# Re-ordering the work ahead of the first head step in an AdaLN, attention and routed-FFN kernel

## The reference

```python
# block 1 (the part that the change touches)
scale, shift = split(emb @ W_emb + b_emb)
xn  = rms_norm(x, g_norm) * (1 + scale) + shift
q, k, v = heads(xn @ W_qkv)                 # 16 heads of 32
q, k = rms_norm(q, g_q), rms_norm(k, g_k)   # per head
o   = softmax(q k^T * 32**-0.5) v           # 512 x 512 per head, no mask
y   = o + o @ W_out
# block 2: latent attention with rotary parts and a causal mask
h   = y + attention(rmsnorm(y))
# block 3: one shared expert, and 2 of 7 routed experts per token
out = x + h + moe(rmsnorm(h))
```

## Time and profile before

| | |
|---|---|
| median of 3 runs | 1350.78 us (1350.34 to 1356.07) |
| the profiled execution | 1353.06 us |
| its span, first to last instruction | 1351.3 us |
| TensorE busy in the span | 1200.8 us (89%) |
| VectorE, ScalarE, GpSimd busy | 738.7, 576.2, 296.2 us |
| mean granted TensorE clock | 0.959 of full |

### The profile page before, as it was taken

The page is one execution under the profiler, slowest core; times in us unless marked ns, Lnnn a source line. Parts: engine busy times, 40 slices in busy tenths (PEclk is TensorE's granted clock), DMA queues, the critical chain, the costliest instruction groups (busy, mean ns, idle before and its releaser), DMA issues.

```text
span 1351.3 us, 18930 instructions
## 1 busy us (share of the span) xinstructions
PE 1200.8 (89%) x6315; PEld 860.4 (64%) x6315; DVE 738.7 (55%) x1548; ACT 576.2 (43%) x1248; POOL 296.2 (22%) x244
## 2 busy tenths in 40 slices
PE   4857989999999889999999989989988898999970
PEld 4734655665566456558668767766656687888860
DVE  4346386467545765655465375465354675444432
ACT  3215365435433554554454454454364653222210
POOL 2312222100210021001011100200124344555530
PEclk9968999999999999999999899998999998999995
DMA  6062243224311731442365263354448623655669
GB/s 244 1 187 91 74 133 109 79 76 161 110 45 63 229 95 48 145 157 76 109 204 165 67 206 122 83 192 139 123 161 298 212 86 94 110 110 110 111 125 332
DMA packets 88030, 178.43 MB, mean 132 GB/s; under 512 B 12512, under 2 KB 23168, under 8 KB 86400
## 3 DMA queue, kind: packets, MB, share of 16 engines
q1 hardware_dynamic: 79424, 157.29, 36.1%
q0 software_dynamic: 8512, 19.93, 7.9%
HBM read 111.64 MB, written 65.27 MB: 131 GB/s over the span
## 4 chain that ended last, share of the span: by engine, by line
PE 75%; DVE 10%; DMA 5%; ACT 4%; issue 4%; SPq 1%; POOL 1%; ACTq 0%; DVEq 0%; POOLq 0%
PE psum L841 13%; PE psum L658 9%; PE psum L660 7%; PE psum L659 7%; PE psum L825 6%; PE psum L801 6%; PE psum L667 3%; PE psum L918 3%; PE psum L920 3%; PE psum L919 3%; DVE nmax L1547 2%; PE psum L945 2%; PE psum L887 2%; PE psum L947 2%; PE psum L946 2%
## 5 line engine op out<-in xcount | busy, mean ns | idle before, releaser
L1137 ACT ACTIVATE probs<-psum 128x512 f32<-128x512 f32 (+3 forms) x512 | 256.3, 516 | 241.9 <-PE psum L828 128.3
L1547 DVE TENSOR_REDUCE nmax<-psum 128x1 f32<-128x512 f32 (+3 forms) x512 | 290.5, 585 | 120.9 <-PE psum L801 86.4
L825 PE MATMUL psum<-stack 97*128 97x512 f32 (+3 forms) x512 | 204.2, 400 | 27.5 <-ACT probs L1137 18.8
L801 PE MATMUL psum<-stack 96*128 96x512 f32 (+3 forms) x512 | 211.5, 418 | 6.4 <-DMA stack<-split_s 6.4
L841 PE MATMUL psum<-probs,vals 128*33 128x512 f32 (+3 forms) x1024 | 210.5, 533 | 0.0
L825 PEld LDWEIGHTS psum<-stack 97*128 97x128 f32 x512 | 99.6, 195 | 49.0 <-ACT probs L1137 27.2
L801 PEld LDWEIGHTS psum<-stack 96*128 96x128 f32 x512 | 101.2, 198 | 39.8 <-issue 28.4
L841 PEld LDWEIGHTS psum<-probs,vals 128*33 128x33 f32 x1024 | 49.6, 112 | 99.7 <-issue 69.3
L658 PE MATMUL psum<-w_hi,xh 128*128 128x512 f32 (+1 forms) x256 | 95.2, 372 | 7.3 <-POOL xl L1239 5.6
L659 PE MATMUL psum<-w_hi,xl 128*128 128x512 f32 (+1 forms) x256 | 93.6, 366 | 0.0
L660 PE MATMUL psum<-w_lo,xh 128*128 128x512 f32 (+1 forms) x256 | 93.6, 366 | 0.0
(11 more groups left out here) (236 smaller groups left out, 2372.5 us busy)
## 6 DMA issues: line engine op xcount, KB each, us to landing
stack<-split_s SPq DMA_DIRECT2D x384, 128.0 KB, 3.0
split_s<-split SPq DMA_DIRECT2D x64, 512.0 KB, 2.8
xt<-in_x_dram SPq DMA_DIRECT2D x4, 1024.0 KB, 5.8
x_s<-yt SPq DMA_DIRECT2D x4, 1024.0 KB, 5.0
xt<-x_s SPq DMA_DIRECT2D x4, 1024.0 KB, 4.8
yt<-in_x_dram SPq DMA_DIRECT2D x4, 1024.0 KB, 5.5
res<-x_s SPq DMA_DIRECT2D x4, 1024.0 KB, 9.6
acc_s<-yt SPq DMA_DIRECT2D x4, 1024.0 KB, 5.9
```

The lines of the kernel that those rows point to most:

```text
L801: last = nc.tensor.matmul(psum[:, bank, 0:n], st[:, 0, t * P:(t + 1) * P], st[:, 1, 0:n], start=True, stop=not causal)
L825: last = nc.tensor.matmul(psum[:, bank, lo:S], st[:, 1, t * P:(t + 1) * P], st[:, 0, lo:S], start=True, stop=not causal)
L1137: sk.cleared(nc.scalar.activation(probs[:, M % NX, lo:S], psum[:, sk.bank(M), lo:S], ACT.Exp, scale=SCALE), M)
L1547: sq.cleared(V.tensor_reduce(nmax[:, M // STEPS_P % 2, c:c + 1], psum[:, sq.bank(M), 0:n], AX.X, ALU.max, negate=True), M)
```

## The change

Six things change, all ahead of the first head step or in the first round.

1. All four low parts of Wqkv are made by VectorE, ahead of its wait for the modulation product. GpSimd makes none.
2. The first `qk` product no longer waits for all of x and Wqkv: before each of its four chunks TensorE waits for the chunk's x and low part alone.
3. Values later: after the `qk` products come `hnorm` and `hscale` of group 0, then `v` 0 to 2, `turn` q and `turn` k of group 0, `v` 3, then `hscale` and `turn` of group 1.
4. The RMS norm of sequence 1 moves from the head steps 4 to 11 of round 0 in among the `qk` products (after `qk` 2, 5 and 6); SP loads that x ahead of its stores.
5. Pair 0 is not read back from DRAM. SP and ScalarE copy it from `split` straight into `stack`, with 12 DMAs of 64 KB (SP head 0, ScalarE head 1; each 3 for k, 3 for q). The stores of group 0 still run, for pair 1. ScalarE waits for these 12 copies before it overwrites `split` with group 1.
6. `turn_max(0)` comes after `scores` 9 in place of after `scores` 13, and ScalarE issues the DMA of its row in place of SP.

Small things: the router weights' split moves to later points of `FIRST`.

```diff
@@ before_heads(j)
+    square, norm, scale = normalize(j + 1)
     for n in range(2 * NT):
         keys += [("qk", j, n)] + ([("hsum", j, n - 1)] if n else [])
-    keys += [("hsum", j, 2 * NT - 1)] + [("v", j, t) for t in range(NT)] + [("hnorm", j, n) for n in range(4)]
-    for g in range(2):
-        keys += [("hscale", j, g, c) for c in "kq"] + [("turn", j, g, c) for c in "kq"]
-    return keys
+        keys += {2: square, 5: norm, 6: scale}.get(n, [])
+    keys += [("hsum", j, 2 * NT - 1)] + [("hnorm", j, n) for n in range(4)] + [("hscale", j, 0, c) for c in "kq"]
+    keys += [("v", j, t) for t in range(NT - 1)] + [("turn", j, 0, c) for c in "qk"] + [("v", j, NT - 1)]
+    return keys + [("hscale", j, 1, c) for c in "kq"] + [("turn", j, 1, c) for c in "qk"]
@@ beside_heads(k)
     if k == 0:
-        square, norm, scale = normalize(j)
-        put((4, 5, 6, 7), square)
-        put((8, 8, 9, 9), norm)
-        put((10, 10, 11, 11), scale)
@@ waits on the stack
-            eng.wait_ge(stack_ld[p % 4], 96 * (p // 4 + 1))
+            eng.wait_ge(stack_ld[p % 4], 96 * (p // 4 + (1 if p % 4 else 2)))
+        FIRST_PARTS, FIRST_SIDE = {"k": {0: 2, 1: 2, 2: 3}, "q": {0: 0, 1: 1, 2: 0}}, {"k": 1, "q": 0}
@@ SP
+            def place_first(c):
+                for role in FIRST_PARTS[c]:
+                    sp.dma_start(stack[DH * role:DH * role + DH, FIRST_SIDE[c], 0, :].bitcast(F32),
+                                 split[0:DH, FIRST_PARTS[c][role], :].bitcast(F32)).then_inc(stack_ld[0], 16)
...
-            for g in range(2):
-                store_k(0, g)
-                store_q(0, g)
-                for a in range(2):
-                    load_pair(0, 2 * g + a)
             load_x(1)
-            place_rows(0)
+            store_k(0, 0)
+            place_first("k")
+            store_q(0, 0)
+            place_first("q")
+            load_pair(0, 1)
+            store_k(0, 1)
+            store_q(0, 1)
+            for q in (2, 3):
+                load_pair(0, q)
@@ TensorE
+            def first_chunk_ready(c):
+                pe.wait_ge(v_lo, VALUE_NO["x", 0, c] + 1)
+                pe.wait_ge(w1_lo, c + 1)
...
-                        product(key, tokens(t), w1(c * D, D))
+                        product(key, tokens(t), w1(c * D, D), None if at_[0] or j else first_chunk_ready)
...
             for M in range(LEAD):
                 scores(M)
-            turn_max(0)
+                if M == STEPS_P + 1:
+                    turn_max(0)
@@ ScalarE
                     g, c = at_
+                    if NG * j + g == 1:
+                        wait_stack(act, 0)
...
+            def place_first(c):
+                for role in FIRST_PARTS[c]:
+                    act.dma_start(stack[DH * role:DH * role + DH, FIRST_SIDE[c], 1, :].bitcast(F32),
+                                  split[DH:2 * DH, FIRST_PARTS[c][role], :].bitcast(F32)).then_inc(stack_ld[0], 16)
...
             for key in FIRST[NT:]:
                 beside(key)
-                if key == ("x", 0, NC - 1):
+                if key == ("turn", 0, 0, "k"):
+                    ring.wait_read(act, key)
+                    place_first("k")
+                    act.wait_ge(v_lo, VALUE_NO["turn", 0, 0, "q"] + 1)
+                    place_first("q")
+                if key == ("v", 0, 0):
                     act.wait_ge(rw_ok, 1)
                     copy(rwh[:, :, :], rwt[:, :, :]).then_inc(rw_hi, 1)
             max_rows(0)
+            ring.wait_read(act, ("max", 0))
+            act.dma_start(stack[XSTACK:XSTACK + 1, 0, 0:2, :].bitcast(F32).rearrange("a h (t c) -> a (h t) c", c=P),
+                          mrow[0:2 * NT, :].bitcast(F32)).then_inc(rows_ld[0], 16)
@@ GpSimd
-            for c in (1, 3):
-                pool.wait_ge(w1_hi, c + 1)
-                nc.gpsimd.tensor_tensor(w1l[:, c, :], w1_raw[:, c, :], w1h[:, c, :].bitcast(F32),
-                                        ALU.subtract).then_inc(w1_lo, 1)
@@ VectorE
             for key in FIRST[NT:3 * NT]:
                 beside(key)
+            for c in range(NC):
+                dve.wait_ge(w1_hi, c + 1)
+                V.tensor_tensor(w1l[:, c, :], w1_raw[:, c, :], w1h[:, c, :].bitcast(F32), ALU.subtract).then_inc(w1_lo, 1)
             dve.wait_ge(mod_mm, 1)
...
-            for c in (0, 2):
-                dve.wait_ge(w1_hi, c + 1)
-                V.tensor_tensor(w1l[:, c, :], w1_raw[:, c, :], w1h[:, c, :].bitcast(F32), ALU.subtract).then_inc(w1_lo, 1)
```

More of the change, by code:

```diff
@@ L653, in _, with three @@
         def _(pe):
-            def three(out, lhs, rhs):
+            def three(out, lhs, rhs, ready=None):
                 n = len(lhs)
                 for i, ((ah, al), (bh, bl)) in enumerate(zip(lhs, rhs)):
+                    if ready:
+                        ready(i)
                     nc.tensor.matmul(out, ah, bh, start=(i == 0), stop=False)
@@ L668, in turn, with product @@
                 ring.filled(last, key)
-            def product(key, lhs, rhs):
+            def product(key, lhs, rhs, ready=None):
                 ring.wait_free(pe, key)
                 n = rhs[0][0].shape[-1]
-                ring.filled(three(psum[:, ring.bank(key), 0:n], lhs, rhs), key)
+                ring.filled(three(psum[:, ring.bank(key), 0:n], lhs, rhs, ready), key)
+            def first_chunk_ready(c):
+                pe.wait_ge(v_lo, VALUE_NO["x", 0, c] + 1)
+                pe.wait_ge(w1_lo, c + 1)
             def chans():
@@ L713, in beside @@
                     if j < B:
-                        if at_[0] == 0:
+                        if at_[0] == 0 and j:
                             pe.wait_ge(v_lo, VALUE_NO["x", j, NC - 1] + 1)
-                            if j == 0:
-                                pe.wait_ge(w1_lo, NC)
-                        product(key, tokens(t), w1(c * D, D))
+                        product(key, tokens(t), w1(c * D, D), None if at_[0] or j else first_chunk_ready)
                     elif c == 0:
@@ L1572, in _ @@
                 beside(key)
-                if key == ("x", 0, NC - 1):
+                if key == ("hnorm", 0, 3):
                     dve.wait_ge(v2_ld, 64)
                     dve.sem_inc(rw_ok, 1)
+                if key == ("turn", 0, 0, "k"):
                     dve.wait_ge(rw_hi, 1)
```

## The result

The changed kernel takes 1329.23 us (median of 4 runs, 1327.75 to 1332.91) against 1350.71 for the kernel before: ratio 0.9836, interval 0.9804 to 0.9868. Timed again in five rounds it gave 0.9840 (0.9809 to 0.9872). The forecast was 1327, with 1322 to 1336 as its range. The profiled execution has a span of 1328.2 us; before it was 1351.3.

The account below looks back on a forecast made before the run. TensorE was taken to bound the whole run (89% busy), with holes at the front. Gains of 17.4 us up to scores_t(0) and 6.3 in round 0 sum to 23.7; from the median, 1350.78 - 23.7 = 1327, range 1322 to 1336.

Parts of the forecast that it names:

- Low parts: Wqkv low parts made before VectorE's wait for the modulation product: x starts at 29.3 in place of 32.28, 3.0 us gained.
- Chunks: First qk product by chunks: last chunk starts at 36.2, product ends at 37.3 in place of 43.7; 6.4 us gained so far.
- Values later: Before the head steps: turn q at 64.5, its low part ending at 68.2; the fourth v costs nothing.
- Direct copies: Pair 0 straight into the stack, 0.43 us per issue, landing 2.85: first scores at 74.1 in place of 85.5, 11.4 gained.
- Row of maxima: Row issued at 81.8, landing in 2.6 us: scores_t(0) at 84.4 in place of 101.8, 17.4 gained.
- rival B: Before scores_t(0), the row of maxima waits for the loads around it, landing in 5.67: 3.1 us less gain, 1330; chance 0.12.
- Round 0: Steps 0 to 17: shorter step 12 wait (3.8), less time at the lower clock (1.8), shorter VectorE queue (0.7): 6.3 us.
- A: Rival, pair 0's copies: ScalarE issues as slowly as GpSimd, 1.59 us each; scores 4.9 late, 1332; chance 0.10.
- C: Rival, steps 0 to 17 of round 0: nothing gained there, another wait fills step 12; 1333 us; chance 0.10.
- D: Rival: no change, the front's gain is taken back by a later wait that doesn't move; 1350 us; chance 0.03.
- E: Rival: slower, pair 0's direct copies are the bottleneck at 6.78 us per issue; scores 36 later, 1363; chance 0.03.
- the signs of being wrong: First scores after 79, over 4 us from the row's issue to scores_t(0), or over 2 us waiting on stack at step 2.

Follow-up runs that it names:

- The undoing run: Changed kernel with the RMS norm of sequence 1 again beside head steps 4 to 11 of round 0; scores_t(0) to first qk of sequence 1: 33.61 against 28.04 us.

## Why the prediction was right

The chain that it named was the right one. The gain, 21.5 us, lies 2.2 under its 23.7, but that closeness is in part luck. Up to Q, where the chain ends, the changed kernel gained 18.3 (18.9 in its repeat), 5 under the forecast. The rest came behind Q, where nothing was changed, and did not come again: from Q to the end it is 1217.1 before, 1212.3 in the changed kernel's first profile and 1218.0 in its repeat. Timed again, the medians differ by 19.6. By the prediction's own steps:

*Low parts (3.0 forecast).* x's first value at 29.58, 2.7 gained; undoing it cost 2.6.

*Chunks (3.4 more).* Undoing them cost 3.1 at C. What I had missed is in the row at 33.52: the first matmul waited 0.94 for VectorE, not for GpSimd. The product's bank is that of x's third transpose, and is free only when the third value has been read. I had the start at 32.1. From 33.52 on TensorE never waited for a chunk: seven steps of 0.43 kept it busy until each was there, so the last low part, which I had as the limit, was not one here. It was in the three profiles in which all of the product's matmuls took 0.23. There TensorE waited between the chunks, as in the run with pair 0 through DRAM:

```profile
36.70 0.50 PE L666 MATMUL psum<-w_hi,xh 128*128 128x512 f32 x1 [0.28 <-POOL xl L1258]
```

This is the last chunk (36.2 forecast), and C was 37.7, only 0.4 earlier. The gain at C was 5.8, not 6.4.

*Values later.* `turn` q came 27.0 after C; 27.2 had been worked out from the end of the first product. The fourth `v` lay in idle time; worth 2.4.

*Direct copies: the step that failed.* I took 0.43 for an issue on both queues and let 1.7 us come from skipping DRAM (5.0 forecast between C and the first scores, less 2.7 for the fourth `v` and 0.6 for GpSimd's quicker low part). The issues took 0.51 to 1.88, 0.88 on average on ScalarE. The 512 KB stores between the copies are a part of it, as the run with the copies first shows: ScalarE's six took 5.26 with them and 4.12 without, where I had 2.6. The first scores came 8.8 earlier, not 11.4, and the new wait behind them put the first maximum 1.64 behind the scores in place of 0.80 (I had allowed 2.1). Together the part cost 1.1 to 1.8 where I had counted on a small gain. The range for the price of ScalarE's issue, 0.43 to 1.59, held it (0.88).

*Row of maxima.* `turn_max` and the changed queue are worth 3.9, the x load's new place 1.9. The landing took 3.7 where I took 2.6, inside the bounds 2.4 to 5.67. The prediction's "six more" maxima was wrong, though its sum, which goes by the 93.65 of the row, does not use it. Here rival B had the mechanism, and with it the rule quoted from the Trainium skill ("DMA: Bandwidth & Descriptors", "Issuing engines are not separate DMA queues"). With the loads of pairs 2 and 3 kept away the row landed 1.8 sooner; so they held it up, though it was issued from another queue, and issued by SyncE it landed no later (3.65). The trace agrees with the rule. The same rule says that issuing from two engines saves only issue time; 12 copies issued in 4.1 us, against 12 loads in 5.5 on one queue, do not speak against it.

*Round 0.* 6.3 forecast. The undoing run gives 5.6 to 7, with the 3.60 wait to the hundredth. In the changed kernel's own profile only 4.4 showed; its repeat had a stretch of 26.8, which makes it 5.6. The term was some 0.7 too large, or more.

The terms at T, from the runs: low parts 2.6, chunks 2.7, values 2.4, row of maxima 3.9, x load 1.9, direct copies -1.8: together 11.7 of the 13.9 that T moved. Some 0.5 of the rest is GpSimd's low part of q, 1.29 where it was 1.83; the other 1.7 was not taken apart and stays open. Parts that share a wait need not add up.

Of the 23.1 us by which the spans of the two profiles differ, 18.3 lie before Q. The other 4.8 came with no change in the order of work behind Q, and are scatter: over all fourteen profiles the time from Q to the end goes from 1206.0 to 1219.6. A part may be clock: in this window of 300 us it was 0.96 before (first row) and 0.98 after; over the whole stretch behind Q it reads 0.97 in both.

```profile
700.00:1000.00 300.00, 280.67 (x1779) 210.11 (x1777) 162.22 (x411) 141.46 (x354) 31.69 (x32) 0.96 0.43 134
700.00:1000.00 300.00, 278.92 (x1775) 206.27 (x1774) 159.00 (x403) 141.99 (x352) 35.25 (x34) 0.98 0.46 146
```

Of the rivals, B and A each came true by a little over a third of their price (a landing of 3.72 between 2.6 and 5.67; an issue of 0.88 between 0.43 and 1.59). C, D and E did not occur, and none of the signs of being wrong did.

## What to carry to other kernels

Follow the start-up as a chain from queue to queue, and for each transfer ask what megabytes stand ahead of it: here a load moved out of the way (1.9) and a transpose that no longer stood behind scores it did not need (2.3 of 3.9) were worth more than a shorter route for the data. Skipping DRAM is no gain by itself when it takes twice as many DMAs and makes the next group wait for them. When single executions scatter by 12 to 15 us, judge a front of 100 us by marks in the trace, relative to the last thing that both versions share.

## What was not expected of the hardware

The direct copies, issued on two queues at once, took longer to issue than loads on one: 0.63 us on SyncE and 0.69 on ScalarE (6 and 6 copies of 64 KB), against 0.46 on SyncE alone (12 loads of 128 KB). Which of the two differences it is stays open. With 512 KB stores between the copies single issues reached 1.70 and 1.88. A long issue needs no second queue, though: in the run with x's load first, where SyncE is the only one to issue, one load of pair 2 took 1.46, some 4 us behind the stores of group 1.

The row of maxima, 4 KB, landed within 1.9 us of its issue with no load in flight, in 3.1 to 3.8 beside or behind the 12 loads of pairs 2 and 3, in 4.6 behind 18 loads, and in 5.7 with the load of the next x put between.

The spread of executions goes with the mean granted clock. Of the changed kernel's six timed executions the quickest, with a span of 1321.0, had 0.971, and the slowest, 1333.3, 0.962; of the kernel before, 1345.4 had 0.964 and 1360.0 had 0.955. In each pair 0.01 of clock goes with 14 to 16 us, somewhat more than the 12 that it would be if all that TensorE does (1200 us) were longer by that share. That the clock is the cause is not shown: less idle time of TensorE would go with both.
